# A delta-rule attention and mixture-of-experts layer: 16x16 inversions merged by matmuls, values convolved channel-major, a bias product over 128 rows, and a new order of steps

## The reference

```python
# block 1: H = 8 heads of 128, on h = layernorm(x)
mixed = causal_depthwise_conv(h @ qkv_w.T, taps=4)      # 3072 channels: q, k, v
beta  = sigmoid(h @ b_w.T)
alpha = exp(-exp(A_log) * softplus(h @ a_w.T + dt_bias))
for t in range(T):                                      # per head, S is 128 x 128
    S = S * alpha[t]
    S = S + outer(k[t], (v[t] - k[t] @ S) * beta[t])
    o[t] = q[t] @ S
x = x + (rmsnorm(o) * norm_w * silu(h @ z_w.T)) @ out_w.T
# block 2: router, top 2 of 8 experts, each relu(h @ W1 + b1) @ W2 + b2
x = x + sum over the 2 experts of weight * expert(layernorm(x))
```

## Time and profile before

| | |
|---|---|
| runs | 1421.86 us median (1419.13, 1422.89, 1421.86) |
| profiled execution, span | 1397.9 us (no time of its own is given; 24.0 us less than the median) |
| TensorE busy | 1199.9 us (86%), 12203 products |
| VectorE | 1164.4 us (83%), 2531 |
| ScalarE | 832.0 us (60%), 2536 |
| GpSimd | 707.9 us (51%), 598 |
| DMA | 97.1 MB, 163176 packets, of them 115623 under 512 bytes |

### The profile page before, as it was taken

One profiled execution on the slowest core, in us unless ns is written; L12 is line 12 of the kernel. 1 busy time (PEld: TensorE's weight loads), 2 busy tenths in 40 slices (PEclk: granted clock), 3 DMA queues, 4 the chain that ended last, 5 costly groups with the idle time before them and its releaser, 6 DMA issues.

```text
span 1397.9 us, 34191 instructions
## 1 busy us (share of the span) xinstructions
PE 1199.9 (86%) x12203; PEld 944.0 (68%) x12203; DVE 1164.4 (83%) x2531; ACT 832.0 (60%) x2536; POOL 707.9 (51%) x598
## 2 busy tenths in 40 slices
PE   0355999999999999999999999999999989479991
PEld 0233868686868687777777777777777767358881
DVE  6878898989898998989898989897989783578875
ACT  1252666666666666657566666756566655358884
POOL 3151727464555656473828292928192822235552
PEclk9997999999999999999999999999999998789996
...
GB/s 208 0 98 32 73 35 73 47 69 62 54 63 53 62 54 64 52 68 48 84 34 91 28 98 25 103 28 88 30 85 43 73 55 98 104 96 78 76 65 181
DMA packets 163176, 97.10 MB, mean 69 GB/s; under 512 B 115623, under 2 KB 148269, under 8 KB 161988
## 3 DMA queue, kind: packets, MB, share of 16 engines
...
## 4 chain that ended last, share of the span: by engine, by line
DVE 37%; PE 21%; POOL 17%; issue 10%; DMA 9%; SPq 3%; ACT 3%; POOLq 0%; DVEq 0%; ACTq 0%
DVE blkT L1060 9%; POOL kq L637 9%; DVE Y_sb L1056 9%; DMA blkN<-scr_n 4%; PE kx L1553 3%; POOL decay L629 3%; POOL rows_in L609 2%; DVE Gs L1204 2%; POOL kq L620 2%; DMA scr_n<-area 2%; PE rc L1717 2%; SPq L477 2%; DVE blkN L1047 1%; DVE area L1170 1%; DVE Y_sb L1043 1%
## 5 line engine op out<-in xcount | busy, mean ns | idle before, releaser
L637 POOL TENSOR_TENSOR kq<-tapA,area 128x256 f32<-128x256 f32 x256 | 252.0, 998 | 93.6 <-DVE area L1146 92.8
L758 ACT ACTIVATE area<-pj,taps 128x256 f32<-128x256 f32 x256 | 123.1, 481 | 142.7 <-PE pj L1567 136.5
L1056 DVE TENSOR_TENSOR Y_sb<-blkT,blkN 128x4 f32<-128x4 f32 (+18 forms) x304 | 169.5, 558 | 10.5
L609 POOL DMA_INDIRECT rows_in<-rowbuf,dest x64 | 64.6, 1009 | 202.1 <-DVE dest L1132 175.2
L1143 DVE SCALAR_TENSOR_TENSOR tapA<-pj,taps,tapA 128x256 f32<-128x256 f32 x256 | 122.2, 477 | 53.4 <-ACT tapA L758 51.6
L1553 PE MATMUL kx<-kq 128*128 128x128 f32 x1024 | 141.0, 285 | 20.0 <-ACT area L767 9.6
L1553 PEld LDWEIGHTS kx<-kq 128*128 128x128 f32 x1024 | 128.7, 197 | 38.4 <-issue 21.8
L620 POOL TENSOR_TENSOR kq<-kq,area 128x1024 f32<-128x1024 f32 x64 | 151.1, 2362 | 0.0
L1060 DVE TENSOR_REDUCE blkT<-Y_sb 128x2 f32<-128x4 f32 (+18 forms) x304 | 142.4, 469 | 5.2
L758 ACT ACTIVATE tapA<-pj,taps 128x256 f32<-128x256 f32 x256 | 123.0, 480 | 0.0
L1146 DVE SCALAR_TENSOR_TENSOR area<-pj,taps,area 128x256 f32<-128x256 f32 x256 | 121.4, 474 | 0.0
...
## 6 DMA issues: line engine op xcount, KB each, us to landing
...
scr_n<-area SPq DMA_DIRECT2D x128, 32.0 KB, 1.6
...
```

The costliest lines, as they stand in the source:

```text
L637: nc.gpsimd.tensor_tensor(dst[:, n % H, :], tapA[:, n % RING, :], tapB[:, n % RING, :], ALU.add).then_inc(conv_done, 1)
L758: ins = nc.scalar.activation(dst[:, n % RING, :], pj[n % 2][:, k:k + GT], ACT.Copy, scale=taps[:, t, k:k + 1])
L1056: ins = nc.vector.tensor_tensor(p4, bc(blkT[:, r0:, j:].rearrange("p r (o m) -> p r o m", o=1), [128, nr, w, wd]), bc(blkN[:, j:j + w, j:] ...
```

## The change

Five parts. (1) The inversion works on 16x16 blocks: of each 32x32 block the two diagonal 16x16 blocks are inverted (the upper one in partitions 0 to 63, the lower in 64 to 127), in a solve of 8 products and 8 sums in place of 19 and 19, and a copy turns the result. Two products on 32-row strips (`y16`, `r16`, 64 each), a ScalarE copy (`ye`) and four VectorE reads (`re`) make the off-diagonal 16x16 block; the blocks now arrive in R, and `td` transposes three of the four 32x32 blocks into T64. Out go three transfers, in come eight. (2) Values are convolved like keys and queries: heads 16 to 23 of `proj`, `taps`, `first`, `last` into vT, and `v` is four transposes per half chunk. The folding of taps into weights is gone. (3) The bias product has 128 rows, 126 of them zero. (4) ORDER is written anew, with 11 parts of `inv` for 22. (5) The stand-in products are gone. The diff, cut:

```diff
-    NT = 2 * H
+    NT = 3 * H
...
-        order = [H + h for h in range(H)] + list(range(H))
-
-        PAIR0 = 6
-        SOLVE = [(j, 2) for j in range(BLK - 2, PAIR0 - 2, -2)] + [(j + i, 1) for j in range(PAIR0 - 2, -2, -2) for i in range(2)]
-        INV = 5 + 2 * len(SOLVE)
+        order = [H + h for h in range(H)] + list(range(H)) + [2 * H + h for h in range(H)]
+
+        SOLVE = list(range(SUB - 2, -2, -2))
+        INV = 6 + 2 * len(SOLVE)
...
-            proj.0 proj.1 taps.0 taps.1 diag.0 first.0 v.0.0 proj.2 m.1.0 taps.2 al.0 first.1 proj.3 m.0.0 last.0 taps.3
...
+            proj.0 sm first.0 ka.0 y16 taps.0 first.1 proj.1 ye re al.0 last.0 r16 taps.1 td.0 v.0.0 taps.2 first.2
...
+                            half_ = slice(SUB * side, SUB * side + SUB)
+                            sp.dma_start(blkN[64 * side:64 * side + 64, :, :], scr_n[:, half_, half_]).then_inc(blk_in, 16)
...
-                        sp.dma_start(scr_t.rearrange("q (a p) m -> p q a m", p=2)[0], blkT[0:64, :, :]).then_inc(t_out, 16)
+                        sp.dma_start(scr_r[:, 0:SUB, 0:SUB], blkR[0:64, :, :]).then_inc(t_out, 16)
+                        sp.dma_start(scr_a, blkT[0:64, :, :]).then_inc(t_out, 16)
                     elif step == "ti" and a is not None:
-                        sp.wait_ge(s_scr, 32)
-                        sp.wait_ge(t_out, a * 32 + 32)
+                        sp.wait_ge(s_scr, 48)
+                        sp.wait_ge(t_out, a * 48 + 48)
+                        if g is not None:
+                            sp.wait_ge(u_mm, halves(g, GC - 1, U - 1))
+                        for b in range(NB):
+                            sp.dma_start(TA[BLK * b:BLK * b + SUB, :, :], a_blocks[b]).then_inc(t_in, 16)
                         for b in (0, 1):
                             r = slice(BLK * b, BLK * b + BLK)
-                            sp.dma_start(T64.rearrange("p g h c -> p (g h) c")[r, :, r], inverses[b]).then_inc(t_in, 16)
+                            sp.dma_start(Rq[r, :, r], r_blocks[b]).then_inc(t_in, 16)
...
+                            act.dma_start(Rq[r, :, r], r_blocks[b]).then_inc(t_in, 16)
...
-            for k in range(TAPS):
-                nc.gpsimd.tensor_tensor(wv_taps[k], wv_raw, tap_rows[:, :, k], ALU.mult).then_inc(s_fold, 1)
...
+                        if n // H == 2 and g is not None:
+                            pool.wait_ge(v_mm, g * HALVES + U * (GC - 1) + n % H // HU + 1)
...
-                nc.scalar.activation(wv_hi[:, k, :], wv_taps[k], ACT.Copy, scale=-VSCALE).then_inc(s_vhi, 1)
...
+                    if step == "ye":
+                        act.wait_ge(blk_mm, 2 * g + 1)
+                        nc.scalar.activation(Y16.rearrange("p q j -> p (q j)"), ob[1][:, 0:GC * H * SUB], ACT.Copy).then_inc(y16_sb, 1)
...
-                nc.vector.scalar_tensor_tensor(out=wv_lo[:, k, :], in0=wv_taps[k], scalar=-VSCALE, in1=wv_hi[:, k, :],
...
+                flat = blkN.rearrange("p a b -> p (a b)")
+                diag = flat[:, 0:SUB * SUB:SUB + 1]
-                coupling = blkN[:, :, :].rearrange("p a b -> p (a b)")[:, 1:BLK * BLK:2 * BLK + 2]
-                full = prod[:, 0:BLK // 2 * BLK].rearrange("p (a b) -> p a b", b=BLK)
+                coupling = flat[:, 1:SUB * SUB:2 * SUB + 2]
+                full = prod[:, 0:SUB // 2 * SUB].rearrange("p (a b) -> p a b", b=SUB)
                 if s == 0:
-                    ins = nc.vector.tensor_copy(blkT[:, :, :], par_eye[:, :, :])
+                    ins = nc.vector.memset(blkT.rearrange("p a b -> p (a b)"), 0.0)
                 elif s == 1:
+                    nc.vector.memset(blkT.rearrange("p a b -> p (a b)")[:, 0:SUB * SUB:SUB + 1], 1.0)
                     dve.wait_ge(blk_in, a * 32 + 32)
                     ins = nc.vector.memset(diag, 0.0)
                 elif s == 2:
                     ins = nc.vector.tensor_tensor(full, pairs[:, :, 1, :],
-                                                  bc(coupling.rearrange("p (i o) -> p i o", o=1), [128, BLK // 2, BLK]),
+                                                  bc(coupling.rearrange("p (i o) -> p i o", o=1), [128, SUB // 2, SUB]),
                                                   ALU.mult)
+                elif s == INV - 1:
+                    ins = nc.vector.tensor_copy(blkR[:, :, :], blkT.rearrange("p r j -> p j r"))
                 else:
-                    j, w = SOLVE[(s - 5) // 2]
-                    r0, wd = (j + 1) // 2, BLK - j
-                    nr = BLK // 2 - r0
-                    p4 = prod[:, 0:nr * w * wd].rearrange("p (r k m) -> p r k m", k=w, m=wd)
+                    j = SOLVE[(s - 5) // 2]
+                    n = SUB - 1 - j
+                    p4 = prod[:, 0:n * 2 * n].rearrange("p (r k m) -> p r k m", k=2, m=n)
                     if s % 2 == 1:
                         ins = nc.vector.tensor_tensor(
-                            p4, bc(blkT[:, r0:, j:].rearrange("p r (o m) -> p r o m", o=1), [128, nr, w, wd]),
-                            bc(blkN[:, j:j + w, j:].rearrange("p (o k) m -> p o k m", o=1), [128, nr, w, wd]), ALU.mult)
+                            p4, bc(blkT[:, j + 1:, j + 1:].rearrange("p r (o m) -> p r o m", o=1), [128, n, 2, n]),
+                            bc(blkN[:, j:j + 2, j + 1:].rearrange("p (o k) m -> p o k m", o=1), [128, n, 2, n]), ALU.mult)
                     else:
-                        ins = nc.vector.tensor_reduce(blkT[:, r0:, j:j + w], p4, AX.X, ALU.add, negate=True)
+                        ins = nc.vector.tensor_reduce(blkT[:, j + 1:, j:j + 2], p4, AX.X, ALU.add, negate=True)
...
+                            dve.wait_ge(y64_mm[c], rounds(g))
...
+                    if step == "re":
+
+                        dve.wait_ge(blk_mm, 2 * g + 2)
+                        for b in (1, 3, 0, 2):
+                            top = slice(BLK * b, BLK * b + SUB)
+                            ins = nc.vector.tensor_single_scalar(
+                                Rq[top, :, BLK * b + SUB:BLK * b + BLK],
+                                ob[1][top, GC * H * SUB:2 * GC * H * SUB].rearrange("p (q j) -> p q j", j=SUB), -1.0, ALU.mult)
+                        ins.then_inc(r16_done, 1)
+                    elif step == "td":
+
+                        dve.wait_ge(r16_done, rounds(g))
+                        for b in ((0, 2), (1,))[arg[0]]:
                             band = slice(BLK * b, BLK * b + BLK)
-                            ins = nc.vector.transpose(R[band, :, :, band], T64[band, :, :, band] if b < 2 else T32[band, :, :, :])
-                        ins.then_inc(rdiag, 1)
+                            ins = nc.vector.transpose(Tq[band, :, BLK:2 * BLK] if b == 1 else Tq[band, :, 0:BLK], Rq[band, :, band])
+                        ins.then_inc(t_diag, 1)
...
-                ("kq", 0, 1): (("z", 0, 0), pj[0], 7),
-                ("gt", 0, 0): (("z", 0, 0), pj[0], 8),
...
+            def small_blocks(g, a, r, step):
+
+                bank_free((step,), g, a, r)
+                n = GC * H * SUB
+                if step == "y16":
+                    pe.wait_ge(t_in, g * (32 * NB) + 32 * NB)
+                    y = ob[1][:, 0:n].rearrange("p (q j) -> p q j", j=SUB)
+                    for q in range(GC * H):
+                        for b in range(NB):
+                            r_ = slice(BLK * b, BLK * b + BLK)
+                            ins = mm(y[r_, q], Nm[r_, q // H, q % H, r_], TA[r_, q, :], start=True, stop=True)
+                    ins.then_inc(blk_mm, 1)
...
+                else:
+                    pe.wait_ge(y16_sb, rounds(g))
+                    y = ob[1][:, n:2 * n].rearrange("p (q j) -> p q j", j=SUB)
+                    for q in range(GC * H):
+                        for b in range(NB):
+                            r_ = slice(BLK * b, BLK * b + BLK)
+                            ins = mm(y[BLK * b:BLK * b + SUB, q], Y16[r_, q, :], Rq[r_, q, BLK * b + SUB:BLK * b + BLK], start=True, stop=True)
+                    ins.then_inc(blk_mm, 1)
...
-                        w = slice(512 * u, 512 * u + 512)
-                        for k in range(TAPS):
-                            cols = ds(column(g, c) - PAD + k, C)
-                            hi, lo = xflat(xn_hi)[:, cols], xflat(xn_lo)[:, cols]
-                            mm(rc[u][:, :], hi, wv_hi[:, k, w], start=(k == 0), stop=False)
-                            mm(rc[u][:, :], hi, wv_lo[:, k, w], start=False, stop=False)
-                            mm(rc[u][:, :], lo, wv_hi[:, k, w], start=False, stop=False)
+                        pe.wait_ge(conv_done, tile(g, 2 * H + HU * u + HU - 1))
+                        for h in range(HU):
+                            ins = mm(heads(rc[u])[:, h, :], vT[:, HU * u + h, C * c:C * c + C], ident[:, :], start=(h == 0), stop=False,
+                                     is_transpose=True)
+                        ins.then_inc(v_mm, 1)
...
```

(2 more changed lines are left out.)

197 lines of the change are left out of this document (104 added, 93 removed).

## The result

The changed kernel takes **1508.13 us** (median of 4, 1503.77 to 1510.84) against 1422.34 us before: 1.0597 times as long, interval 1.0568 to 1.0625. 1290 was forecast, with 0.05 on slower. The profiled execution took 1506.71 us for a span of 1504.6, so 2.1 us lie around the span. The 24.0 us of the forecast were no such thing: on the chips of all later comparisons the unchanged kernel before has a median of 1399 to 1403 us, which fits the span of its profile, 1397.9 us. The 1422 us were measured on another chip. So ratios are compared here, each with the kernel before on the same chip.

The account below looks back on a forecast made before the run. VectorE was taken to set the 67.25 us round, falling to 60.2. Savings of 106 (rounds) + 4 + 9 (start) - 1 (last stage) + 14 (experts) = 132 off the 1397.9 us span, plus 24.0 around it, gave 1290 us; range 1250 to 1350.

Parts of the forecast that it names:

- What bounds the kernel now: Opening step: VectorE, 60.66 us busy, sets the 67.25 us round with 6.6 idle; TensorE has some 44 us of issue.
- The terms of TensorE: TensorE per round: less 10.4 and 3.2 us, plus 2.7, 1.8 and 2.2, so 44 us of issue becomes 37.
- forecast 51.9 us: VectorE's work per round: 60.7 - 16.0 (inversion) + 6.3 (value heads) + 1.6 (PSUM reads) - 0.7 (transposes).
- Rival (3), the lock: GpSimd's eight additions block VectorE through the shared SBUF port: round 64.1 us, about 1350; 0.25 together with the transfers rival.
- The second ring: Loop of mask, block transfers, inversion and merges through VectorE: pieces together 67.3 us a round, forecast to become 58.1.
- rival (2): Block transfers around the inversion cost 7.7 us more instead of 2: ring 64.0, total 1346; 0.25 together with the lock rival.
- Rival (5), a falling clock: TensorE drops to 1.2 GHz throughout, 37 us becoming 74: 1500 us; decides once over 30 us run low; chance 0.04.
- a granted clock of 0.5 inside a round: Listed sign that the forecast is wrong: TensorE's clock at 0.5 in the rounds, where 1.00 was expected.
- Small blocks 1.1 us: In the ring behind the inversion: 64 products of one 32-row block at 0.033 us a pair, 1.1 us, twice.
- The stand-ins: TensorE's 15 filler products of 512 columns in each round, whose removal was counted as 3.2 us less issue.
- Start: Before the rounds: first convolution at about 73 instead of 77.14 us, 4 us less; first stage 9 us less.
- Experts: Experts' tiles, bound by TensorE: the 128-row bias product takes them from 3.40 to 3.0 us, saving 14 us (5 to 16).

Follow-up runs that it names:

- a_same: The changed kernel run again with nothing altered, on a later chip: 1.038 times the kernel before on that chip, rounds of 71.33 us.
- b_inv16: The kernel before with the 16x16 inversion alone, in the old order: ratio 1.084 to the kernel before, rounds of 74.95 us.
- a_stand2: The changed kernel with 14 stand-in products filling TensorE's wait ahead of the first gated half: ratio 1.026 to the kernel before, rounds of 70.84 us.
- b_nostand: The kernel before without its 15 stand-in products: ratio 1.009 to the kernel before, rounds of 68.49 us.
- a_quarter: The changed kernel with three of four bands of the small block products left out after the first round: ratio 1.032 to the kernel before, rounds of 70.33 us.
- a_dense: The changed kernel with a 256-column product after every fourth small product of the first block step: ratio 1.061 to the kernel before, rounds of 73.55 us.

## Why the prediction was wrong

**What bounds the kernel now: the step that failed.** The prediction gave TensorE 44 us of issue in a round and said that VectorE sets it. The rate was right, the count was not: "160 of 128 columns in fp32, taken at the same 0.11" are 288. TensorE's lines in the very round of the earlier trace rows:

```profile
L1553 PE MATMUL kx<-kq 128*128 128x128 f32 x64 | 8.5, 279 | 1.1 <-POOL kq L637 0.5 <-ACT area L767 0.4 <-ACT GTs L841 0.3
L1603 PE MATMUL rc<-w_hi,xn_hi 128*128 128x512 f16 x16 | 6.1, 380 | 0.0
L1621 PE MATMUL rc<-rhs,area 128*128 128x128 f32 x32 | 4.3, 277 | 0.0
```

The 160 calls are 128 products and 32 transposes. A product in fp32 stands in the trace twice, as two passes, a transpose once: L1553 64, L1621 and five lines like it 32 each, and two lines of transposes 16 each, 288 in all. In order of time eight such passes take 0.9 to 1.0 us from start to start:

```profile
641.80 1.13 PE L1621 MATMUL rc<-rhs,area 128*128 128x128 f32 x8
642.76 1.06 PE L1553 MATMUL kx<-kq 128*128 128x128 f32 x8
643.66 0.61 PE L1621 MATMUL rc<-rhs,area 128*128 128x128 f32 x4
```

288 x 0.111 = 32 us in place of 17.8; with the merges' passes counted too TensorE issues some 60 us in a round of 67.25. It was as full as VectorE, and in order. The terms of TensorE, the idle time kept at VectorE's 6.6 us and the price put on holes all rest on this count. The change leaves TensorE 304 such passes (34 us), 72 of 259 columns (8), 12 gate products (2.6), 256 small ones (2.5) and some 7 of merges and others: 54 us, not 37. That still fits into 60.2, but only if TensorE has hardly a hole. In eight rounds of a_same it has 9.7 us idle a round and a clock of 0.93, 10 us of a round at the lower level, half of them lost:

```profile
316.50:895.80 579.30, 500.90 (x7182) 441.37 (x7181) 454.80 (x1028) 400.02 (x1261) 344.03 (x316) 0.93 0.23 52
```

54 + 10 + 5 = 69 of 71.3 us; where the rest lies is not shown. Of the idle time the wait for the normalised output is 3.8 us (60.9 / 16) and the pauses in the small products are 2.8.

**Point by point.**

- VectorE: forecast 51.9 us, measured 55.6. The inversion costs 9.2 us, not 6.7: L1075 and L1079 take (58.0 + 41.7) / 16 = 6.2 us where 5.2 was the sum, the steps before and the copy 3.0 where 1.5 was. Its saving is 13.5 us, and it buys little while TensorE is full.
- Rival (3), the lock, has its mechanism in these 2.5 us. In the first stage, with GpSimd idle, the inversion's steps take what the sum had. In a round the first of them ends just after the operation of GpSimd beside it:

```profile
93.34 0.29 DVE L1061 TENSOR_TENSOR prod<-blkN 128x128 f32<-128x128 f32 x1
...
664.26 1.90 POOL L662 TENSOR_TENSOR S<-S,a_end 128x1024 f32<-128x1024 f32 x1 [7.13 <-PE ob L1694]
664.74 1.57 DVE L1061 TENSOR_TENSOR prod<-blkN 128x128 f32<-128x128 f32 x1
```

L1065 goes from 0.29 to 0.70 us in the same way, the product of 2 elements from 0.16 to 0.62, that of 18 from 0.18 to 0.48, that of 338 from 0.51 to 0.75, each time only where an operation of GpSimd runs beside it: 2.4 us a round on average. The convolutions, which read PSUM and one buffer, keep their 0.48 us, as the prediction said against this rival. So its place was the inversion and not the additions, its size 2.4 and not 5.6 us.
- The second ring, which "takes just as long", was no evidence. Its four pieces are cut between events of consecutive rounds, so they add up to the period whatever bounds it. The mask at 688.54, where the ring was closed, did not wait for the merges alone: on VectorE it comes right behind the scan, without idle time.
- The transfers, rival (2), do not hold the changed order: in a_same the blocks are back at about 609 us, and TensorE takes them up at 613.53. In the old order it waited for them (b_inv16, 3.8 us in the round shown).
- Rival (5), a falling clock, given 0.04 and 1500 us, named the right engine, and its time is near the measured one by luck. Its mechanism is there in part: the clock is 0.50 for 7 us in a round of a_same and averages 0.91 over the first profile's rounds. But it needed 30 us at the low level; it decided earlier, since TensorE had no spare 23 us to lose it from. Holding the clock in one hole gives back 0.6 to 1.3% (a_stand2); it is not the whole loss. The sign that the text named ("a granted clock of 0.5 inside a round") came true, as did VectorE's wait before L1209 (up to 10.2 us).
- "Small blocks 1.1 us" for each step was a bare sum of rows. The passes themselves hold it, 128 in 1.26 us with the tail of the last, but the pauses in the run of 256 short passes with their weight loads cost 2.4 to 3.9 us a round more, by chip. The Trainium skill (TensorE: Matmul & The Clock Gate, Wait — 56ns, not 53.3ns?) puts a floor of about 25 ns under the step from one start to the next. By it the 128 passes would take 3.2 us; in these rows they take less than half of that between pauses.
- The stand-ins were taken off TensorE as 3.2 us saved. b_nostand shows the opposite, about 1 us a round lost.
- Start: the first convolution comes at 65.12 instead of 77.14 us, 12 us earlier (4 forecast); the first opener 10.9 earlier. With the first stage, 13 were forecast.
- Experts: from 3.40 to 3.0 us a tile forecast; 3.21 and 3.22 over all steps on the later chips, 4.04 on the first. Last stage: 1 us forecast, 13 to 17 lost; its clock is 0.72 there against 0.82. Which hand-off costs them was not tried.

**What is shown and what stays open.** Shown: in the old order the 16x16 inversion alone costs 5 to 8 us a round, though it frees VectorE of 12 us; the value part, taken out of the changed kernel, gains 5.5; the bias part gains 0.6%; work added to TensorE lengthens the changed round more than work added to VectorE. Argued from sums, not isolated: that the inversion's loss is the small passes, their pauses and the clock. Open: why time taken off TensorE comes back so poorly (a_quarter, 1.0 of 3.6 us), which speaks for hand-offs between the engines as a second bound; how much of the loss is the new order itself (it can't be taken out alone, since the steps need it); and why the pauses in short products and the stalls of every third tile differ by chip. The pauses come after some 150 short passes, each with a weight load (a_same, b_inv16), in the first chip's round above already after 33, and go when longer products stand between them (a_dense). That points to the supply of instructions, but no run isolates it.
